# High one-hots of an edge row made by four compares with one value a partition instead of one compare of two tensors

## The reference, cut to what matters

```python
norm_x = weight * (x * rsqrt(mean(x * x) + EPS))
out = norm_x @ W_root + bias
for r in range(2):                       # two relations
    w = (edge_type == r)
    msg = norm_x[src] @ W_rel[r] * w[:, None]
    sums = segment_sum(msg, dst, num_segments=N)
    cnt = segment_sum(w, dst, num_segments=N)
    out = out + sums / maximum(cnt, 1.0)[:, None]
y = elu(out) @ wo
```

## Time and profile before

| | us |
|---|---|
| median of 3 runs (625.84 to 626.62) | 625.91 |
| the profiled execution | 625.88 |
| its span, first to last instruction | 624.1 |
| PE busy in the span | 575.7 |
| DVE busy in the span | 420.2 |
| ACT busy | 200.7 |
| POOL busy | 107.5 |

### The profile page before, as it was taken

One profiled execution on the slowest core, in us unless ns is written; L12 is line 12 of the kernel. 1 busy time (PEld: TensorE's weight loads), 2 busy tenths in 40 slices (PEclk: granted clock), 3 DMA queues, 4 the chain that ended last, 5 costly groups with the idle time before them and its releaser, 6 DMA issues.

```text
span 624.1 us, 8374 instructions
## 1 busy us (share of the span) xinstructions
PE 575.7 (92%) x2581; PEld 397.9 (64%) x2581; DVE 420.2 (67%) x1028; ACT 200.7 (32%) x417; POOL 107.5 (17%) x109
## 2 busy tenths in 40 slices
PE   0399999999997999999999999999999989989991
PEld 0355555555556767676788898886878855544450
DVE  6668888888885588888732212017847666799777
ACT  9133333333311355554322221012223222132322
POOL 9600000000000000001146333301202220033120
PEclk9999999999999899999999999999999999999997
DMA  9111111111102112122820000510100100022113
GB/s 271 51 34 34 34 33 33 33 33 33 33 1 87 34 34 66 34 67 78 227 104 0 0 0 1 164 47 2 35 0 0 34 1 0 1 66 66 55 44 98
DMA packets 21727, 30.72 MB, mean 49 GB/s; under 512 B 6281, under 2 KB 15987, under 8 KB 21696
## 3 DMA queue, kind: packets, MB, share of 16 engines
q1 hardware_dynamic: 21542, 30.07, 15.9%
q10 hardware_dynamic: 154, 0.26, 0.1%
HBM read 25.20 MB, written 5.12 MB: 49 GB/s over the span
## 4 chain that ended last, share of the span: by engine, by line
PE 85%; DVE 11%; issue 1%; ACT 1%; DMA 1%; POOL 1%; SPq 0%; DVEq 0%; POOLq 0%
PE banks L665 19%; PE banks L807 11%; PE banks L726 11%; PE banks L889 8%; PE banks L638 6%; PE banks L696 5%; PE banks L819 4%; PE banks L829 4%; PE banks L755 4%; PE banks L757 4%; PE banks L736 3%; PE banks L879 2%; PE banks L700 2%; PE banks L646 1%; PE banks L711 1%
## 5 line engine op out<-in xcount | busy, mean ns | idle before, releaser
L665 PE MATMUL banks<-w_all,xnT 128*125 128x429 f32 x320 | 130.0, 528 | 0.0
L665 PEld LDWEIGHTS banks<-w_all,xnT 128*125 128x125 f32 x320 | 54.1, 189 | 29.0 <-issue 28.3
L889 PE MATMUL banks<-wd_s,dT 128*125 128x512 f32 x160 | 70.4, 595 | 1.9 <-DVE s L1299 1.0
L726 PE MATMUL banks<-hT,w_s 128*128 128x250 f32 x320 | 68.7, 375 | 0.4 <-DVE hT L1186 0.3
L726 PEld LDWEIGHTS banks<-hT,w_s 128*128 128x128 f32 x320 | 60.3, 189 | 9.1 <-issue 2.2
L638 PEld LDWEIGHTS banks<-oh_code,oh_low 125*128 125x128 bf16 x320 | 31.3, 98 | 45.6 <-issue 43.7
L755 PE MATMUL banks<-y_hi,adj 125*125 125x288 f32 x200 | 56.5, 309 | 0.4 <-DVE small L1102 0.4
L638 PE MATMUL banks<-oh_code,oh_low 125*128 125x240 bf16 x320 | 48.1, 272 | 8.2 <-issue 8.2
L757 PE MATMUL banks<-y_lo,adj 125*125 125x286 f32 x200 | 54.7, 299 | 0.0
L889 PEld LDWEIGHTS banks<-wd_s,dT 128*125 128x125 f32 x160 | 29.5, 187 | 38.1 <-issue 35.0
L340 POOL TENSOR_SCALAR xh<-x_first,small 125x1024 f32<-125x1024 f32 x6 | 7.4, 1241 | 268.2 <-DVE adj L1130 268.1
(11 more groups left out here) (187 smaller groups left out, 903.5 us busy)
## 6 DMA issues: line engine op xcount, KB each, us to landing
xt<-in_x SPq DMA_DIRECT2D x20, 448.0 KB
out_x<-ot SPq DMA_DIRECT2D x9, 448.0 KB
w_s<-in_L_gnn_W SPq DMA_DIRECT2D x5, 512.0 KB, 6.4
w_all<-in_L_gnn_W_rel SPq DMA_DIRECT2D x2, 1144.0 KB, 10.8
wd_s<-in_L_gnn_Wd SPq DMA_DIRECT2D x1, 2048.0 KB, 12.5
w_all<-in_L_gnn_W_root SPq DMA_DIRECT2D x1, 1144.0 KB, 7.9
xt<-in_x SPq DMA_DIRECT2D x20, 52.0 KB
wo_s<-in_L_gnn_wo_weight SPq DMA_DIRECT2D x1, 1024.0 KB
```

The source lines that it names most:

```text
L665: ins = pe.matmul(pb[0:P, 2 + 2 * v + n, 0:FH], xnT[:, u], w_all[:, u, n * FH:(n + 1) * FH], start=(u == 0), stop=(u == KD - 1))
L726: ins = pe.matmul(pb[:, 4 + f % 2, 0:2 * P], w1_s[:, k, f * 128:(f + 1) * 128], hT[:, k], start=(k == 0), stop=(k == KD - 1))
L889: ins = pe.matmul(pb[0:P, 2 + 2 * u + q], dT[:, k, u * P:(u + 1) * P], wd2_s[:, k, q * 512:(q + 1) * 512], start=(k == 0), stop=(k == K1 - 1))
```

## The change

The table `iota_c` loses its last axis: the numbers 0 to 239 stand once and side by side, where each stood twice. The high one-hots are laid out column by column, [2 buffers, 4 columns, 240], so that the 240 elements of a column are neighbours, where they were 2 elements apart; the count matmuls stream them as rows without gaps. The codes of the edges are kept as f32 in a tensor of their own (`code`) instead of f16 in one with the low numbers, which takes one clear more (and a smaller clear of `edge`). `codes` is now four tensor_scalar instructions of 240 elements, each comparing the table with one f32 value a partition; it was one tensor_tensor of 960 elements that compared two tensors. The far part (`codeS`) is not run for these inputs.

```diff
-             ("oh_low", [P, 2, H, LOW, JH], BF16), ("oh_code", [P, 2, H, R * C, JH], BF16),
-             ("iota_c", [P, R * C, JH], F16), ("iota_l", [P, LOW, JH], F16), ("iota_i", [128, 1], F32),
-             ("edge", [P, 2, GP, J], F16), ("farE", [P, 2, GP, J], F32),
-             ("codeF", [P, GP, J], F16), ("lnw", [128, KD], F32),
+             ("oh_low", [P, 2, H, LOW, JH], BF16), ("oh_code", [P, 2, J, R * C], BF16),
+             ("iota_c", [P, R * C], F16), ("iota_l", [P, LOW, JH], F16), ("iota_i", [128, 1], F32),
+             ("edge", [P, GP, J], F16), ("code", [P, GP, J], F32), ("farE", [P, 2, GP, J], F32),
+             ("lnw", [128, KD], F32),
...
-            pool.iota(iota_c[:], [[1, R * C], [0, JH]], base=0, channel_multiplier=0,
+            pool.iota(iota_c[:], [[1, R * C]], base=0, channel_multiplier=0,
...
-                                        oh_code[:, b, q, :, j], start=(j == 0), stop=(j == JH - 1))
+                                        oh_code[:, b, q * JH + j], start=(j == 0), stop=(j == JH - 1))
...
             dve.memset(edge[:], 0.0)
+            dve.memset(code[:], 0.0)
...
-                dve.tensor_copy((edge, farE)[f // 2][:, f % 2, 0:G],
+                dve.tensor_copy((edge[:, 0:G], code[:, 0:G], farE[:, 0, 0:G], farE[:, 1, 0:G])[f],
...
-            def codes(g, b, code):
-
-                return dve.tensor_tensor(oh_code[:, b], both(iota_c, R * C), spread_out(code, g, R * C), ALU.is_equal)
+            def codes(g, b, a):
+
+                for j in range(J):
+                    ins = dve.tensor_scalar(oh_code[:, b, j], iota_c[:],
+                                            a[:, bass.ds(g, 1), j:j + 1].rearrange("p o j -> p (o j)"), None, ALU.is_equal)
+                return ins
...
-                codes(g, g, edge[:, 1]).then_inc(onehots, 1)
+                codes(g, g, code).then_inc(onehots, 1)
...
-                    codes(g + 2, u % 2, edge[:, 1]).then_inc(onehots, 1)
+                    codes(g + 2, u % 2, code).then_inc(onehots, 1)
```

More of the change, by code:

```diff
@@ L94, in graph_kernel @@
         p1 = base
-        (w_all, xn, xnT, oh_low, oh_code, iota_c, iota_l, iota_i, edge, farE, codeF, lnw,
+        (w_all, xn, xnT, oh_low, oh_code, iota_c, iota_l, iota_i, edge, code, farE, lnw,
          mini, small1, signs), end1 = stack(p1, [
              ("w_all", [128, KD, FW], F32), ("xn", [P, D], F32), ("xnT", [128, KD, P], F32),
-             ("oh_low", [P, 2, H, LOW, JH], BF16), ("oh_code", [P, 2, H, R * C, JH], BF16),
-             ("iota_c", [P, R * C, JH], F16), ("iota_l", [P, LOW, JH], F16), ("iota_i", [128, 1], F32),
-             ("edge", [P, 2, GP, J], F16), ("farE", [P, 2, GP, J], F32),
-             ("codeF", [P, GP, J], F16), ("lnw", [128, KD], F32),
+             ("oh_low", [P, 2, H, LOW, JH], BF16), ("oh_code", [P, 2, J, R * C], BF16),
+             ("iota_c", [P, R * C], F16), ("iota_l", [P, LOW, JH], F16), ("iota_i", [128, 1], F32),
+             ("edge", [P, GP, J], F16), ("code", [P, GP, J], F32), ("farE", [P, 2, GP, J], F32),
+             ("lnw", [128, KD], F32),
              ("mini", [1, GP * H], I32), ("small1", [P, 8], F32), ("signs", [1, 8], F32)])
@@ L1000, in lows @@
             def lows(g, b):
-                return dve.tensor_tensor(oh_low[:, b], both(iota_l, LOW), spread_out(edge[:, 0], g, LOW), ALU.is_equal)
-            def codes(g, b, code):
-                return dve.tensor_tensor(oh_code[:, b], both(iota_c, R * C), spread_out(code, g, R * C), ALU.is_equal)
+                return dve.tensor_tensor(oh_low[:, b], both(iota_l, LOW), spread_out(edge[:], g, LOW), ALU.is_equal)
+            def codes(g, b, a):
[3 more added lines that the diff above has]
+                return ins
             for g in range(2):
                 lows(g, g)
-                codes(g, g, edge[:, 1]).then_inc(onehots, 1)
+                codes(g, g, code).then_inc(onehots, 1)
             crowds = [0]
@@ L1088, in far_counted @@
                         dve.wait_ge(s_codes, w * 4 + 2)
-                        dve.tensor_tensor(codeF[:], codeS[:], maskS[:, 1], ALU.add).then_inc(s_codes, 1)
+                        dve.tensor_tensor(codeS[:], codeS[:], maskS[:, 1], ALU.add).then_inc(s_codes, 1)
                         dve.tensor_scalar(dist, dist, -float(W), None, ALU.add).then_inc(s_codes, 1)
@@ L1093, in far_counted @@
                             lows(g, 0)
-                            codes(g, 0, codeF).then_inc(s_onehots, 1)
+                            codes(g, 0, codeS).then_inc(s_onehots, 1)
                             dve.wait_ge(s_counts_mm, w * G + g + 1)
```

## The result

The changed kernel takes **631.75 us** (median of 4 runs, 631.27 to 632.44) where the kernel before, beside it on the same chip, takes 625.88 (625.44 to 626.62): ratio 1.0093, 95% interval 1.0076 to 1.0111. It is slower by 5.9 us; 6.1 were forecast.

The account below looks back on a forecast made before the run. TensorE set the pace before; in the loop VectorE's sequencer was to become the bound. Start -1.3, two early rows +0.4 and loop +7.0 sum to +6.1 on 625.9, so 632.0 us, range 624.4 to 638.5.

Parts of the forecast that it names:

- (a): Start: halving iota_c's elements saves GpSimd time at 5.4 ns an element, so -1.3 us (bounds -0.96 and -1.3).
- (d): Unrolled tiles: longer VectorE rows hidden behind TensorE, except the two rows ahead of them, +0.4 us.
- (b): High one-hots on VectorE's engine: four compares at a step of 0.19 us each, +0.20 us a row.
- The fixed part: In a compare's step on VectorE: 0.07 us beside the streaming, read from the add of 240 elements.
- the pointer: In a compare's step on VectorE: 0.06 us for its pointer scalar, read from the L1186 instructions.
- the two halvings: In a compare's streaming: one source and 2-byte elements each halve the tick; multiplied, a quarter tick, 0.06 us for 240.
- (c): Loop on VectorE's sequencer: three more register operations, 0.127 us each, make the row 1.91 us and the bound, +7.0 us.
- the lead used up at the loop's entry: Loop: one-hots are ready about 1.2 us ahead before the change; this comes off the loss once.
- (e): TensorE's count matmuls: gapless rows give at most 0.03 us a row, 2.4 in all; taken as nothing.
- Rival 3: Loop: the sequencer's added register operations stay hidden and TensorE keeps the pace, 625.2 us; chance 0.22.
- Rival 1: Loop: VectorE's engine becomes the bound because the halvings don't multiply, row 1.99 us, 637.8 us in all; chance 0.16.
- Rival 4: Loop: sequencer stays hidden and TensorE gains 2.4 us from gapless rows, 622.8 us; chance 0.09.

## Why the prediction was right

The mechanism was right: the loop is bound by the chain on VectorE's sequencer, and the branches lie 33.97 us apart where 33.6 was forecast. That the sum came out within 0.2 us, +6.1 against +5.9, is partly luck. The loop and VectorE's end cost +8.9 and not +7.0; the start gave 1.0 more than forecast; and the first tile gave 1.25, for which the sum had no term and the change no part.

- **(a) The start**: -1.3 forecast, -2.33 measured (the first count's -1.93 less the +0.40 of (d)). The mechanism held: in the kernel before VectorE's pair at L983 ends with the fills, and that end moves by all that iota_c saves. The first count came 1.93 earlier where 0.9 was to be seen. The failed step is the price of 5.4 ns an element. It was read from two rows that both have the repeated inner axis of two, and was applied to one that has none.
- **(b) The step of a compare**: 0.19 forecast, 0.191 measured, record 0.28 and 0.277. The fixed part, the pointer and the two halvings, each read from a different row, held in their sum. The table in four bytes confirms the second halving by itself; the 0.06 of a pointer was not tested alone.
- **(c) The sequencer**: +7.0 forecast, +8.9 measured in the loop's tiles and at VectorE's end (+7.92 and +0.95). A pass is 33.97 instead of 33.6. The plain row is 1.96 instead of 1.91, in part since a led compare costs 0.135 and not 0.127, which had been read from starts known to 0.03 us. This is the term that was sized too small: by the prediction's own scale (+5.3 at 0.12, +7.8 at 0.13) 0.135 gives about +9. The rows with a reciprocal add 0.11 instead of 0.3 each. The splits add 0.97 and 0.77 (0.86 forecast), the loop's turn 0.53 (0.58). Four passes of +2.27 make +9.1 on VectorE; TensorE's eight tiles show +7.92, so the lead used up at the loop's entry was 1.2, as forecast. VectorE's late end cost 0.95 with the last tile, where 0.5 was reckoned.
- **(d) Two rows at the start**: +0.4 forecast, +0.40 measured. The unrolled tiles hide the rest, as forecast; the table in four bytes shows that this cover was thin, for at 2.00 us a row it was gone.
- **(e) TensorE's dense rows**: "none of it while VectorE sets the pace" held for the changed kernel, whose count of four steps 0.41 to 0.42 us with no gain from it. The upper bound behind it was 2.4 us; it is 1.2.
- **Rival 3**, that the sequencer hides it, is refuted by the unrolled version and by the pair with and without an address by g. **Rival 1** asked for a step above 0.21. **Rival 4** is what happens once the sequencer is relieved: 622.6 us measured where it gave 622.8. The agreement is luck: 1.9 of it is the start, where it had 1.3 less 0.4, and the dense rows gave half of its 2.4.
- What was to be seen and wasn't: TensorE's idle time. The prediction looked for some 2 us a pass, over 7 in the 125 us of the window, and TensorE's busy time is short by 3.1 there. The count of matmuls shows the rest, as does the releaser of the weight loads ahead of the counts; the busy time doesn't.

## What to carry to other kernels

An instruction split in four is priced on two lanes: what it takes of the engine (here +0.20 us a row, hidden) and what its addresses take of the sequencer (0.135 us each in a loop, and in program order with every load of a register). Add the sequencer's row up whenever a loop with register addresses also loads registers; it is in no busy share, and it shows as idle time of the engine that "issue" ended. Where it is the bound, unroll, or fetch several rows' registers in one load: here that turns a loss of 0.9% into a gain of 0.4 to 0.6%, about half of which is the earlier start.

## What the runs showed of the hardware

- GpSimd's iota: 240 elements in 0.34 us and 480 in 0.54 when all are running numbers, 256 in 1.47 and 480 in 2.69 with an inner axis of two that repeats each number. That is five times as long for the same 480.
- The TENSOR_LOAD of four values takes 0.344 us, that of two 0.529.
- GpSimd's fills and VectorE's small instructions: the pair of 20 elements that writes y_hi takes 0.23 to 0.29 us behind the fills or beside the last one, and 1.86 or 2.68 when it starts 1.8 or 2.5 us before the fills end.
- TensorE's clock behind the stage. After it TensorE has idle time (1.27 us busy of 4.00 in the first row below), and then in some executions it is granted half the clock (1.2 GHz) for part of the next stretch, so that the mean granted clock of 4 us falls to 0.57. The stretches 199:203 and 203:207 of the kernel before; 203:207 of the kernel with dense rows alone; and 203:207 of the unrolled kernel in its first and in its second profile (199:203 stands at 0.81 in the first and at 1.00 in the second):

```profile
199.00:203.00 4.00, 1.27 (x10) 1.03 (x10) 3.86 (x11) 0.78 (x2) 0.00 (x0) 1.00 0.00 0
203.00:207.00 4.00, 4.00 (x21) 4.00 (x20) 0.31 (x1) 0.52 (x2) 0.00 (x0) 0.57 0.02 4
```

```profile
203.00:207.00 4.00, 4.00 (x21) 2.81 (x20) 1.79 (x6) 0.09 (x1) 0.00 (x0) 1.00 0.01 4
```

```profile
203.00:207.00 4.00, 4.00 (x14) 2.79 (x14) 2.00 (x6) 0.30 (x1) 0.00 (x0) 0.76 0.00 0
```

```profile
203.00:207.00 4.00, 4.00 (x14) 1.78 (x14) 3.36 (x8) 1.64 (x3) 0.00 (x0) 1.00 0.00 0
```

The last two are the same program; its spans are 621.5 and 620.1 us. So 1.4 us between two profiles here can be the clock alone, and a difference of that size is read from the stage's own rows, as it was for the dense rows, and not from the span. It also covers the 0.2 us in the last line of the table above. What decides whether the clock falls was not tried.
